# Local transformer: PE does two q projections of a later window pair ahead of the q.k products

## The chip, the cores and the metric

One NeuronCore of a Trainium2 chip runs the whole program. The metric is the time of one execution on the device, in microseconds (us). PE is TensorE (PEld its weight loads), DVE is VectorE, ACT is ScalarE, POOL is GpSimd, SP the engine that issues the DMAs.

## The reference, cut to what matters

A model of four blocks on x of shape (4, 512, 128); the change touches the third block's feed-forward part, a six-layer local transformer:

```python
DIM, DEPTH, HEADS, DIM_HEAD, WINDOW, QK_SCALE = 128, 6, 16, 64, 32, 8.0
def attn_layer(x, Wqkv, qs, ksc, Wo):
    q, k, v = split(x @ Wqkv)                     # 16 heads of 64
    q, k = l2norm(q) * qs, l2norm(k) * ksc
    q = q * cos * scale + rotate_half(q) * sin * scale
    k = k * cos / scale + rotate_half(k) * sin / scale
    out = local_attention(q, k, v)                # each window of 32 sees itself and the one before, masked
    return out @ Wo
def local_attention(q, k, v):
    sim = einsum('bhwie,bhwje->bhwij', q, k2) * QK_SCALE
    return einsum('bhwij,bhwje->bhwie', softmax(where(mask, -max, sim), -1), v2)
for i in range(DEPTH):
    x = attn_layer(shift_tokens(x), ...) + x
    x = ffn_layer(shift_tokens(x), ...) + x       # layernorm, W1, gelu gate, W2
```

## The kernel before

Each engine has its own in-order queue, written out by hand in `LocalTransformer` (L1612): `tensor` (L1688), `vector` (L1929), `scalar` (L2141), `gpsimd` (L2339) and `sync` (L2425). They meet only in semaphores.

The work of a layer is cut into two half-layers (two of the four batches each), hl = 0 to 11. A half-layer has four blocks u of 128 tokens for two batches, and each block gives two steps g: an even one for the block's windows 1 and 3, an odd one for windows 0 and 2. So a half-layer is eight steps, w = g mod 8, and there are 96 steps. In step g the engines are at different depths of a pipeline:

- PE turns p of g - 1 (`pe_turn_p`, L1820, banks 5 and 6), computes the scores of g (`pe_scores`, L1802: a mask matmul L1811 and 16 small ones L1814, for each of two windows, banks 3 and 4), projects q and k of g + 3 (`pe_rotate`, L1768, four calls i = 0 to 3 into banks 0, 1, 2 and 5; i = 0 and 1 are q, 2 and 3 are k), weighs the values with p of g - 1 (`pe_weigh`, L1831, called the second product), then the output projection of an even step (`pe_project`, L1861) or the value projection of the next block in an odd one (`pe_values`, L1781, L1786 its matmul), and turns q and k of g + 2 (`pe_by_feature`, L1790).
- VectorE copies half of p turned (L2089), takes each window's row maximum and subtracts it (`v_scores`, L2058, L2065 and L2070), multiplies the projections with the rotary tables (`v_rotate`, L1996, L2008 and L2013) and sums squares (L2020), scales q (L2055), sums p's rows and inverts (L2078, L2081).
- ScalarE copies the other half of p turned (L2283), squares the projections (L2229), takes Exp of the scores (L2174), copies the second product's results (L2292) and the values (L2239), places q and k turned (L2253, L2257), and in steps with MLP work does its copies and GELU (L2326, L2328, L2334). It also computes a first guess of roots (L2266, L2268; L2274, L2276 for the MLP).
- GpSimd adds the rotated halves (L2396), scales k (L2403), and scales p by the inverse sums (L2367), which is the event "soft" that `pe_turn_p` of the next step waits for.

The eight PSUM banks are all in use, and each PE call first waits until the bank's last reader is done (`self.freed`). Banks 0 and 1 are freed by ScalarE's placing copies of `pe_by_feature`. The scores wait for these copies too in an even step ("placed"), bank 3 in an odd step for VectorE's residual add (L2096).

The MLP of half-layer hl - 1 lies beside the attention of hl, by a table of places (`beside`, L1671). A place (w, 0) comes in PE's queue between the transposes of p and what the change reorders; the others come later. In w = 5 and w = 6 place (w, 0) turns the rows of the next half-layer (`pe_turn_x`, L1758, recorded at L270), and ScalarE's copies L2221 and L2222 give its columns, the event x_cols. The projections for a new half-layer's first block wait for it:

```python
        if i == 0 and t4 == 0:
            e.wait_ge(*s.at("x_cols", 2 * (2 * hl + bb) + 2))
```

Since the projections run three steps ahead, these are the ones issued in w = 5 and w = 6, each for the batch turned in that same step. The shift matmul of the MLP (`pe_shift`, L1881) ends w = 0; layer statistics (L2104) stand ahead of `v_scores` in w = 1; two MLP transposes (L1891) are in w = 2; MLP-up matmuls (L1902, L1905) in w = 2 to 5; the gate (L2132) ahead of `v_scores` in w = 4 and w = 5, and the down projection (L1917) later in these.

Of the kernel before, what the change touches and what calls it, by code (L numbers as in the profile page):

```python
# [273 lines left out]
def after(e, ends):  # L274
    for sem, value in ends:
        e.wait_ge(sem, value)


class Prologue:
# [61 lines left out]
    def tensor(self, e):  # L341
        pass
# [1269 lines left out]
class LocalTransformer:  # L1612
# [75 lines left out]
    def tensor(self, e):  # L1688
        K, s = self.K, self.s
        after(e, self.before)  # L1690
        e.wait_ge(*s.at("cleared", 3))
        self.freed = {k: [s.at("cleared", 3)] for k in range(8)}
        for bb in range(2):
            self.pe_turn_x(e, 0, bb, 6 + bb)
        for r in range(2):
            for i in range(4):
                self.pe_rotate(e, r, i)
        for n in range(4):
            self.pe_values(e, 0, n)
        for r in range(2):  # L1700
            for i in range(4):
                self.pe_by_feature(e, r, i)
        for i in range(4):
            self.pe_rotate(e, 2, i)
        for g in range(self.NG + 1):
            u, half = divmod(g, 2)
            hl, w = divmod(g, 8)
            this, last, turned, placed = g < self.NG, g >= 1, g + 3 < self.NG, g + 2 < self.NG
            if last:
                self.pe_turn_p(e, g - 1, 0)  # L1710
                self.pe_turn_p(e, g - 1, 1)
            if this:
                self.pe_beside(e, hl, w, 0)
                self.pe_scores(e, g, 0)
                self.pe_scores(e, g, 1)
            if turned:
                self.pe_rotate(e, g + 3, 0)
                self.pe_rotate(e, g + 3, 1)
            if last:
                self.pe_weigh(e, g - 1)  # L1720
            if turned:
                self.pe_rotate(e, g + 3, 2)
                self.pe_rotate(e, g + 3, 3)
            if this:
                self.pe_beside(e, hl, w, 1)
            if half == 0 and last:
                self.pe_project(e, u - 1)
            if half == 1 and this and u + 1 < self.NU:
                for n in range(4):
                    self.pe_values(e, u + 1, n)  # L1730
            if placed:
                for i in range(4):
                    self.pe_by_feature(e, g + 2, i)
            if this:
                self.pe_beside(e, hl, w, 2)
        f = self.NF - 1
        self.pe_shift(e, f)
        self.pe_turn(e, f, 0)
        self.pe_turn(e, f, 1)
        for n in range(6):  # L1740
            self.pe_up(e, f, n)
        self.pe_down(e, f, 0)
        self.pe_down(e, f, 1)
# [902 lines left out]
```

## Time and profile before

| | |
|---|---|
| median of 3 runs | 3143.26 us (3142.95 to 3143.5) |
| the profiled execution's own time | 3143.12 us |
| its span, first to last instruction | 3141.3 us |
| mean granted TensorE clock | 0.885 of full |
| PE busy over the span | 2442.7 us (78%) |
| DVE, ACT, POOL busy | 1963.5 us (63%), 1474.9 us (47%), 1031.8 us (33%) |
| transformer's 96 steps | about 735 to 2722 us |
| PE busy from 735 to 2722 us | 1771.43 of 1987.00 us |

A step is measured from the start of its transposes of p (the last half of them, where they come in two) to the next one's. In half-layer 4, with w = 0 and 1 of half-layer 5:

| w | length, us | end of p's scaling (L2367) to the next transposes, us |
|---|---|---|
| 2 | 19.9 | 0.2 |
| 3 | 19.3 | 2.7 |
| 4 | 25.1 | 5.8 |
| 5 | 23.0 | 2.2 |
| 6 | 17.7 | 0.05 |
| 7 | 16.25 | 0.05 |
| 0 | 21.3 (19.8 in six of eleven half-layers) | 5.1 |
| 1 | 21.5 | 1.3 |

Half-layers 1 to 10 repeat this to within a few tenths, save for w = 0 and what follows it. In half-layer 0, which has no MLP beside it, steps 2 to 4 and 7 take 16.2 to 16.3 us, and steps 5 and 6 take 17.6 and 16.4; the last column is 0.05 to 0.06 there throughout.

A line of the timeline gives the start, the length from first start to last end, the engine, the source line, what is written from what, how many instructions were merged into it, and in brackets how long the engine was idle before it and who ended that.

### The profile page before, as it was taken

To read this page: it belongs to the slowest core of one execution; us is meant where nothing else is said; L and a number is where in the kernel's file an instruction comes from. 1 tells how busy PE (TensorE), PEld (TensorE's weight loads), DVE (VectorE), ACT (ScalarE), POOL (GpSimd) and SP (SyncE) were. 2 spreads that over 40 slices of the span, in tenths; PEclk is the share of its full clock that TensorE was granted. 3 is DMA by queue.
4 is the path that set the end of the run, shared out by engine and by line. 5 is a ranking of instruction groups with operands and counts; after the bars stand their busy time and mean duration, and the time that the engine had idled before them with its cause. 6 is when DMAs were issued, how large, how long until landed. Compare 5 with 4: busy or idle time off the path is not lost. (4 is left out here: it accounts for less than half of the span.)

```text
span 3141.3 us, 71964 instructions
## 1 busy us (share of the span) xinstructions
PE 2442.7 (78%) x30424; PEld 1673.4 (53%) x30424; DVE 1963.5 (63%) x4358; ACT 1474.9 (47%) x2645; POOL 1031.8 (33%) x831
## 2 busy tenths in 40 slices
PE   6817758355889998998989898989898989758463
PEld 3515534233666666565656566656666666535252
DVE  4442235767887877777777868677868777234411
ACT  2303223423556566566656565656565656314120
POOL 0021220004544444444444434443444443000124
PEclk9958868658999999999999999999999999759676
DMA  7001100000101111102101110111100101020022
GB/s 259 3 18 51 34 15 1 0 1 24 29 25 28 53 29 32 29 15 59 29 25 29 53 36 25 28 53 29 32 15 25 35 25 29 15 82 2 9 64 57
DMA packets 71814, 110.10 MB, mean 35 GB/s; under 512 B 11394, under 2 KB 56712, under 8 KB 64966
## 3 DMA queue, kind: packets, MB, share of 16 engines
q1 hardware_dynamic: 67398, 97.88, 11.3%
q0 software_dynamic: 4096, 7.63, 0.8%
q8 instruction: 241, 3.95, 0.5%
q14 instruction: 79, 0.65, 0.1%
HBM read 42.29 MB, written 16.78 MB: 19 GB/s over the span
## 5 line engine op out<-in xcount | busy, mean ns | idle before, releaser
L2396 POOL TENSOR_TENSOR mem<-mem 128x512 f32<-128x512 f32 x384 | 468.0, 1228 | 938.4 <-DVE mem L2013 938.3
L2229 ACT ACTIVATE mem<-ps 128x512 f32<-128x512 f32 x384 | 216.5, 596 | 370.2 <-PE ps L1777 235.2
L1777 PE MATMUL ps<-mem 128*128 128x512 f32 x768 | 383.3, 622 | 4.3 <-DVE mem L2013 2.0
L2253 ACT ACTIVATE mem<-ps 64x512 f32<-64x512 f32 x384 | 228.7, 595 | 143.4 <-PE ps L1798 136.4
L2008 DVE TENSOR_TENSOR mem<-ps,mem 128x512 f32<-128x512 f32 x384 | 257.2, 670 | 22.9 <-ACT mem L2229 22.9
L2013 DVE TENSOR_TENSOR mem<-ps,mem 128x512 f32<-128x512 f32 x384 | 261.0, 680 | 0.0
L1786 PE MATMUL ps<-mem 128*128 128x512 f32 x384 | 208.6, 679 | 55.6 <-ACT mem L2239 55.6
L2020 DVE TENSOR_REDUCE mem<-mem 128x16 f32<-128x1024 f32 x192 | 232.4, 1210 | 0.0
L1848 PEld LDWEIGHTS ps<-mem 64*64 64x64 f32 x12288 | 190.7, 136 | 74.4 <-issue 73.0
L2403 POOL TENSOR_TENSOR mem<-mem 128x1024 f32<-128x1024 f32 x96 | 182.6, 1902 | 132.2 <-DVE mem L2055 132.2
L1814 PEld LDWEIGHTS ps<-mem 128*64 128x64 f32 x6144 | 194.7, 138 | 52.9 <-issue 52.9
L1814 PE MATMUL ps<-mem 128*64 128x64 f32 x6144 | 221.2, 225 | 0.0
L1798 PEld LDWEIGHTS ps<-mem 128*128 128x128 f32 x1536 | 184.7, 148 | 44.3 <-issue 43.6
L1848 PE MATMUL ps<-mem 64*64 64x32 f32 x12288 | 201.9, 220 | 3.5 <-issue 2.7
L1798 PE MATMUL ps<-mem 128*128 128x128 f32 x1536 | 195.5, 283 | 10.4 <-DVE mem L2013 9.7
L2089 DVE COPY mem<-ps 128x512 f32<-128x512 f32 x96 | 66.3, 690 | 217.6 <-PE ps L1826 217.6
L2367 POOL TENSOR_TENSOR mem<-mem 128x1024 f32<-128x1024 f32 x96 | 182.3, 1899 | 32.0 <-DVE mem L2081 32.0
L1777 PEld LDWEIGHTS ps<-mem 128*128 128x128 f32 x768 | 131.1, 190 | 111.7 <-issue 93.2
L1868 PEld LDWEIGHTS ps<-mem 128*128 128x128 f32 x1536 | 180.2, 194 | 19.3 <-issue 11.0
L1868 PE MATMUL ps<-mem 128*128 128x128 f32 x1536 | 181.7, 277 | 2.3 <-ACT mem L2292 2.3
L642 DVE TENSOR_REDUCE mem<-ps 128x8 f32<-128x616 f32 x96 | 76.5, 797 | 170.2 <-PE ps L493 170.2
L2065 DVE TENSOR_REDUCE mem<-ps 128x8 f32<-128x512 f32 x192 | 131.8, 686 | 74.2 <-PE ps L1814 74.0
(286 smaller groups left out, 4591.9 us busy)
## 6 DMA issues: line engine op xcount, KB each, us to landing
mem<-mem SPq DMA_DIRECT2D x48, 768.0 KB, 5.8
mem<-in_Wqkv SPq DMA_DIRECT2D x6, 1536.0 KB, 7.1
mem<-mem SPq DMA_DIRECT2D x36, 256.0 KB, 3.5
x<-mem SPq DMA_DIRECT2D x10, 512.0 KB, 6.5
mem<-x SPq DMA_DIRECT2D x16, 320.0 KB, 5.8
y<-mem SPq DMA_DIRECT2D x16, 320.0 KB, 2.5
mem<-in_W12T SPq DMA_DIRECT2D x8, 512.0 KB, 7.1
mem<-in_L3W SPq DMA_DIRECT2D x16, 256.0 KB, 5.4
```

The lines of the kernel that those rows point to most:

```text
L1777: e.matmul(self.K.ps[:, o, :], self.columns(u, bb), self.K.l2[l % 2]["Wqkv"][:, 512 * i:512 * i + 512], start=True, stop=True, skip_group_ ...
L1786: e.matmul(self.K.ps[:, k, :], self.columns(u, bb), self.K.l2[l % 2]["Wqkv"][:, 2048 + 512 * j:2560 + 512 * j], start=True, stop=True, ski ...
L1798: last = e.transpose(ps[:, o, 128 * c:128 * c + 128], self.T1[r % 2][k][:, h:h + 128], self.K.ident)
L1814: last = e.matmul(ps[64 * bb:64 * bb + 64, k, 64 * c:64 * c + 64], view(self.Qbd[ur][:, bb, c, wn], "p h q -> p (h q)"), self.kT[ur][:, bb ...
L1848: last = e.matmul(ps[64 * hp:64 * hp + 64, 7 - wi, at:at + 32], src[keys, bb, 128 * c + 64 * hp:128 * c + 64 * hp + 64], self.PT[keys, c, ...
L1868: last = e.matmul(ps[:, 3, 128 * bb:128 * bb + 128], self.oT[:, c, bb, :], self.K.l2[l % 2]["Wo"][:, c, :], start=c == 0, stop=c == 7, ski ...
L2008: e.tensor_tensor(h3(t1)[:, hh], src, bc(self.CT[:, t4, k, :], 1, 8), ALU.mult)
L2013: e.tensor_tensor(view(self.T2[:, 512 * j:512 * j + 512], "p (h a c) -> p h a c", h=8, a=2), swapped, bc(view(self.SN[:, t4, k, :], "p (a ...
L2020: e.tensor_reduce(self.ss[bb][:, H * k:H * k + H], h3(self.SQ), AX.X, ALU.add).then_inc(s("square_sums"), 1)
L2229: e.activation(self.SQ[:, 512 * j:512 * j + 512], self.K.ps[:, (0, 1, 2, 5)[i], :], ACT.Square).then_inc(s("squared"), 1)
L2253: e.activation(self.Qbd[ur][q, bb, 4 * j:4 * j + 4, :, hp, :], pv[q], ACT.Copy).then_inc(s("placed"), 1)
L2396: e.tensor_tensor(t1[:, cols], t1[:, cols], self.T2[:, cols], ALU.add).then_inc(s("rotated"), 1)
```

## The change

PE's queue alone is changed: in each step the calls i = 0 and 1 of `pe_rotate` move ahead of both `pe_scores`. Every instruction and every wait stays the same; each wait moves with its instruction.

```diff
             if this:
                 self.pe_beside(e, hl, w, 0)
-                self.pe_scores(e, g, 0)
-                self.pe_scores(e, g, 1)
             if turned:
                 self.pe_rotate(e, g + 3, 0)
                 self.pe_rotate(e, g + 3, 1)
+            if this:
+                self.pe_scores(e, g, 0)
+                self.pe_scores(e, g, 1)
             if last:
                 self.pe_weigh(e, g - 1)
             if turned:
```

## Rows read from the trace of the kernel before

**Rows 1.** The sum of waits, 735 to 2722 us: waiter, releaser, total us, times, longest
```profile
DVE mem L2065 <- PE ps L1814: 74.0, 51, 2.9
...
PE ps L1811 <- ACT mem L2257: 21.8, 25, 1.5
```

**Rows 2.** Timeline of step w = 7 of half-layer 4 and the start of w = 0
```profile
1547.42 1.09 PE L1826 MATMUL ps<-mem 128*128 128x128 f32 x8 [0.58 <-POOL mem L2367]
...
1548.92 0.38 PE L1811 MATMUL ps<-mem 128*128 128x512 bf16 x1 [0.41 <-DVE mem L2096]
...
1550.43 0.69 DVE L2065 TENSOR_REDUCE mem<-ps 128x8 f32<-128x512 f32 x1 [1.05 <-PE ps L1814]
...
1551.72 1.98 PE L1777 MATMUL ps<-mem 128*128 128x512 f32 x4
...
1553.58 0.69 DVE L2008 TENSOR_TENSOR mem<-ps,mem 128x512 f32<-128x512 f32 x1 [0.21 <-ACT mem L2229]
1553.63 2.07 PE L1848 MATMUL ps<-mem 64*64 64x32 f32 x128
...
1561.72 1.90 POOL L2367 TENSOR_TENSOR mem<-mem 128x1024 f32<-128x1024 f32 x1
...
1563.67 1.09 PE L1826 MATMUL ps<-mem 128*128 128x128 f32 x8 [0.70 <-POOL mem L2367]
...
1565.38 0.39 PE L1811 MATMUL ps<-mem 128*128 128x512 bf16 x1 [0.62 <-ACT mem L2257]
```

**Rows 3.** Timeline of step w = 6 of half-layer 4
```profile
1532.37 0.63 PE L270 MATMUL ps<-mem 128*128 128x128 f32 x4 [1.62 <-ACT mem L2257]
...
1532.83 0.38 PE L1811 MATMUL ps<-mem 128*128 128x512 bf16 x1
...
1533.71 0.59 ACT L2222 ACTIVATE mem<-ps 64x511 f32<-64x511 f32 x1
...
1534.34 0.69 DVE L2065 TENSOR_REDUCE mem<-ps 128x8 f32<-128x512 f32 x1 [2.87 <-PE ps L1814]
```

**Rows 4.** Timeline of the end of w = 0 and of w = 1, half-layer 5
```profile
1580.90 0.41 DVE L2096 TENSOR_TENSOR mem<-mem,ps 128x256 f32<-128x256 f32 x1
...
1581.90 2.04 PE L1881 MATMUL ps<-mem 128*128 128x512 f32 x2 [2.50 <-ACT mem L2257]
...
1584.99 1.04 PE L1826 MATMUL ps<-mem 128*128 128x128 f32 x8
...
1585.86 0.38 PE L1811 MATMUL ps<-mem 128*128 128x512 bf16 x1
...
1588.96 0.69 DVE L2065 TENSOR_REDUCE mem<-ps 128x8 f32<-128x512 f32 x1
...
1600.50 3.78 PE L1786 MATMUL ps<-mem 128*128 128x512 f32 x4 [4.23 <-ACT mem L2239]
```

**Rows 5.** Timeline of step w = 2 of half-layer 5
```profile
1616.38 1.07 ACT L2292 ACTIVATE mem<-ps 128x512 f32<-128x512 f32 x2
...
1617.39 1.04 PE L1891 MATMUL ps<-mem 128*128 128x128 f32 x8
```

**Rows 6.** Timeline of step w = 3 of half-layer 5
```profile
1635.60 1.09 ACT L2229 ACTIVATE mem<-ps 128x512 f32<-128x512 f32 x2 [0.40 <-DVE mem L2020]
...
1637.48 3.88 PE L1786 MATMUL ps<-mem 128*128 128x512 f32 x8
...
1646.08 0.66 PE L1826 MATMUL ps<-mem 128*128 128x128 f32 x4 [0.82 <-ACT mem L2326]
```

**Rows 7.** Timeline of step w = 4 of half-layer 5
```profile
1646.57 0.38 PE L1811 MATMUL ps<-mem 128*128 128x512 bf16 x1
...
1649.44 1.89 DVE L2132 TENSOR_TENSOR mem<-mem 128x512 f32<-128x512 f32 x3 [1.98 <-ACT mem L2334]
```

**Rows 8.** Busy time by stretch, w = 0 of half-layers 4 and 5 (stretch, length, PE, PEld, DVE, ACT, POOL busy, PE clock, DMA share, GB/s)
```profile
1400.40:1420.20 19.80, 16.69 (x262) 12.63 (x263) 14.82 (x24) 10.24 (x19) 10.62 (x9) 1.00 0.26 82
1563.67:1584.99 21.32, 18.20 (x263) 13.22 (x263) 14.83 (x24) 10.26 (x19) 10.62 (x9) 0.92 0.15 39
```

## The prediction

> **What bounds the kernel now.** I read three views: who waited for whom over the transformer's stretch, then the timeline of single steps, then granted clock by step. A step is one g of the loop; w is its place (0 to 7) in a half-layer hl (0 to 11), so there are 96 steps.
>
> The sum of waits [rows 1] says that VectorE waits 51 times, 74.0 us in all, for the q.k products, and that PE's first mask matmul of them waits for ScalarE. Both are in the loop that closes in a step with little else in it. Its timeline, w = 7 of half-layer 4 [rows 2]: PE starts the transposes of p at 1547.42, the scores at 1548.92, VectorE's first row maximum follows at 1550.43, and from there VectorE, then GpSimd, run without a gap that matters until p is scaled at 1561.72 + 1.90 = 1563.62. PE's next transposes start at 1563.67, having waited for exactly that. So the period of 16.25 us is a loop: transposes to scores 1.50, scores to maximum 1.51, maximum to p scaled 13.19, and 0.05. PE is busy most of it and still doesn't set it: it had waited 0.70 us when p arrived. Anything that delays the first score in such a step is paid in full.
>
> In other steps PE or ScalarE are late for other reasons, and a later score is free up to a slack that has to be read step by step. That is the whole question here, since the change alters no instruction, only PE's order: the two q projections of g + 3 (four matmuls, 1551.72 to about 1553.65, so 1.93 us [rows 2]) now run ahead of the scores of g. VectorE's, ScalarE's, GpSimd's and SP's queues keep their order, and no DMA moves. The second product starts after the same work as before.
>
> **Step by step.** The transposes take 0.90 us of PE's time (in w = 1, where nothing is waited for, 1584.99 to the scores at 1585.86 [rows 4], 0.87 and a little for the weight load). So in the new order scores start 0.90 + 1.93 = 2.83 us after the transposes, if banks 0 and 1 are free.
>
> *Plain odd steps* [rows 2]: before 1.50, because the scores' bank 3 waits for VectorE's residual add; now 2.83, so +1.33. Against that, VectorE had waited 0.21 us at its first rotate product for ScalarE's square of the same projection; that projection now comes early, and the 0.21 goes. Net +1.1. There are 13 (w = 7 of hl 1 to 10, three in hl 0, which has no MLP beside it): +14.3. The delay also reaches ScalarE's copies of the value products, but PE has the loop's wait to absorb that.
>
> *Plain even steps*: before 1563.67 to 1565.38 = 1.71, the scores waiting for ScalarE's last placing copy. The projections fill this wait instead. 2.83 - 1.71 - 0.21 = +0.9; two in hl 0: +1.8.
>
> *w = 6* [rows 3] is the dear one. Its projections belong to the next half-layer, so the first of them waits for x_cols, which ScalarE makes from transposes that PE does in the same step. These end on ScalarE at 1533.71 + 0.59 = 1534.30. Before, scores (from 1532.83) covered that. Now nothing does: projections from about 1534.4, scores at 1536.3, +3.5, less the 0.2, +3.3. VectorE was waiting for these scores (2.87 us idle), and p's loop closes this step too, so all of it is paid. In hl 0, w = 5 is the same (its MLP-up matmuls, which cover the wait in later half-layers, aren't there). 10 + 2 = 12 times: +39.6. Queued behind the waiting projection are the scores, both second-product groups and the rest of the step; VectorE, then ScalarE's Exp, then GpSimd wait for them.
>
> *w = 0* [rows 4]: same +0.9 on VectorE, but the end is PE's shift matmul, which waits for both ScalarE's copy (just before 1581.90) and VectorE's residual add (1580.90 + 0.41 = 1581.31). The add gets 0.9 later, so the shift about +0.5; 11 times: +5.5.
>
> *w = 1* [rows 4]: layer statistics stand ahead of the maximum on VectorE, so it starts 1588.96 - 1584.99 = 3.97 after the transposes; the first score now is there at 2.83 + 1.51 = 4.34. +0.35, and the chain through Exp to the MLP root carries it on; 11 times: +3.9.
>
> *w = 2* [rows 5]: PE is some 0.8 earlier, because projections fill its wait, but the MLP transposes (1617.39) then wait for ScalarE's output copies, whose last ends at 1616.38 + 1.07 = 1617.45. Gain 0.2; 11 times: -2.2.
>
> *w = 3* [rows 6]: PE-bound, with p scaled 2.7 us before PE comes to it (the table of steps), so the loop itself hides its +1.7. But ScalarE's squares of projections 2 and 3 wait for VectorE: from 1635.60 they go to 1637.3, take 1.09, then two MLP bias copies of 0.69 stand ahead of the first value copy, which starts at about 1639.7 and ends at 1640.3. PE's third value product, due at 1637.48 + 1.93 = 1639.4, needs that bank: +1.0. ScalarE's queue of copies then ends 1.1 later, and the second half of the next transposes (1646.08) waits for it. 11 times: +12.1.
>
> *w = 4 and w = 5* [rows 7]: VectorE does the MLP gate ahead of its maximum, until 1649.44 + 1.89 = 1651.33, which is 4.8 us after PE starts the scores (1646.57) where 1.5 would do: 3.3 us of cover for a delay of 1.9. Nothing. Were the gate gone, they would cost 1.1 each like the rest. Half-layer 11 has no more projections from w = 5 on: nothing.
>
> Sum: 14.3 + 1.8 + 39.6 + 5.5 + 3.9 - 2.2 + 12.1 = 75.0 us.
>
> **The clock.** At the end of w = 0 PE idles 2.50 us ahead of the shift [rows 4]. In five of the eleven half-layers the clock there fell to the lower of its levels (mean 0.92 to 0.95), and w = 0 took some 1.5 us more (21.3 against 19.8) [rows 8]. PE now arrives 0.5 or so earlier (its wait ahead of the scores is filled) and leaves 0.5 later, so it idles about 3.4 us. The unknown is how often the clock falls: bounds are no further case and all six left, 0 to +9; I take +7, since the idle time grows by a third and 4.23 us of idle in w = 1 was followed by value products at half speed (3.78 us for four, against 1.93) [rows 4]. The Trainium skill, TensorE: Matmul & The Clock Gate, section The HAM clock gate, says that the lower clock is the default and activity lifts it; by that rule the sum would go to the upper bound, +9. The trace agrees so far as these rows go.
>
> 75.0 + 7 = +82 on the profiled execution's 3143.12, hence 3225. The median of the runs shown, 3143.26, is the same to 0.01%.
>
> **Rivals.**
> 1. *The clock falls in w = 6 as well.* PE there idles 1.62 us, turns four blocks (0.63) [rows 3], and would idle 1.45 more. At half speed the projections take 1.9 more, and they are on the loop: 12 x 1.9 = 23, so 3248; with the scores slowed too, another 12 x 1 or so, 3260. For: the idle time is near that of w = 0. Against: there is work in the middle, and now, after 1.62 idle, the transposes run at full speed. Chance 0.25.
> 2. *The x_cols wait costs less than I say*, say because ScalarE gets to its two copies sooner, and w = 6 is like a plain step: 12 x (3.3 - 1.1) = 26 less, 3199. The queue order on ScalarE speaks against it. Chance 0.1.
> 3. *Faster: PE's queue is what binds.* If the wait of p's transposes for GpSimd [rows 2] were a coincidence of late PE work, filling PE's wait for ScalarE ahead of the scores would count, 21.8 us in all [rows 1]: 3121. It decides if PE's lag, not p, starts the transposes. It speaks against this that the start is 0.05 us behind GpSimd's end in w = 7 and w = 6 of every half-layer up to 10 (the table). Chance 0.04.
> 4. *The scores' delay is hidden*, VectorE catching up in w = 4 and 5 faster than read; within 0.2%. In the loop-bound steps there is nothing to catch up with. Chance 0.03.
>
> My forecast keeps 0.58. Its own unknowns (w = 3's 12, the clock's 0 to 9, the 0.2 a step) make it 3205 to 3235; taking in rivals 1 and 2, the range is 3192 to 3258. A measurement of this kernel can tell about 0.2%, 6.3 us. Faster 0.04, same 0.03, slower 0.93.
>
> **What would show it.** In w = 7 the scores start 2.83 us after the transposes and the period is 17.3 to 17.4 (16.25 before); VectorE's wait for the scores grows from 74 us to some 150 or more; ScalarE's second x_cols copy turns up as what ends PE's idle time ahead of the projections, 12 times; w = 6 takes 21.0 instead of 17.7 (the table); w = 4 and w = 5 keep their 25.1 and 23.0. Wrong would be: w = 7 unchanged (then the loop isn't one), a w = 6 of 19 or less, or a w = 4 or 5 that has moved by over 0.3.

## The result, and the profile after

| | before | after |
|---|---|---|
| median | 3143.11 us (4 runs, 3140.74 to 3143.5) | 3223.87 us (4 runs, 3221.21 to 3228.56) |
| profiled execution, its span | 3143.12, 3141.3 us | 3221.21, 3219.4 us |
| mean granted TensorE clock | 0.885 | 0.883 |

The ratio is 1.026, with an interval of 1.0242 to 1.0278: slower by 80.8 us between the medians, 78.1 between the profiled executions. The lines of the kernel after are one higher from L1714 on.

The first part of the page of after gives the busy time of the engines:

```profile
PE 2439.6 (76%) x30328; PEld 1682.3 (52%) x30424; DVE 1960.2 (61%) x4358; ACT 1467.4 (46%) x2645; POOL 1032.5 (32%) x831
```

The other engines differ from before by 8 us at most. PE shows 3 us less than before's 2442.7, but 96 of its records are missing, the first mask matmul of each step. Where these records exist they cover 20.3 us of PE's busy time in before, 21.8 in e1 and 14.2 in e4, so by an estimate from these figures PE was busy for 11 to 19 us more than before, and some 59 to 67 of the 78 us are idle time of PE. (The first record of the scores' products, L1815, stands for the start of the scores below.) The sum of waits over the transformer, 735 to 2801 us, in the columns of [rows 1], shows who waits:

```profile
DVE mem L2066 <- PE ps L1815: 174.0, 54, 9.0
...
PE ps L1882 <- DVE mem L2097: 28.1, 10, 3.1
...
PEld ps L1778 <- ACT mem L2223: 23.1, 23, 1.9
...
PE ps L1778 <- ACT mem L2223: 17.0, 13, 1.7
...
PEld ps L1812 <- ACT mem L2258: 1.8, 1, 1.8
```

VectorE's wait for the q.k products grew from 74.0 to 174.0 us [rows 1], the longest from 2.9 to 9.0. L2223 is ScalarE's copy into x_cols, and it ends 13 waits of PE ahead of the projections, 17.0 us: the 12 forecast, and one ahead of the first step. The placing copies can be compared at the weight load of the mask matmul alone, since the matmul's own records are missing. Before, it waited for them 37 times:

```profile
PEld ps L1811 <- ACT mem L2257: 35.0, 37, 1.8
```

and now once (the last row of the block above): the projections stand in these waits.

The timeline of w = 7 of half-layer 4 answers to [rows 2]:

```profile
1591.73 1.10 PE L1827 MATMUL ps<-mem 128*128 128x128 f32 x8 [1.00 <-POOL mem L2368]
...
1592.66 1.88 PE L1778 MATMUL ps<-mem 128*128 128x512 f32 x4
...
1594.69 1.15 PE L1815 MATMUL ps<-mem 128*64 128x64 f32 x32
...
1595.89 0.69 DVE L2066 TENSOR_REDUCE mem<-ps 128x8 f32<-128x512 f32 x1 [2.20 <-PE ps L1815]
...
1598.74 0.68 DVE L2009 TENSOR_TENSOR mem<-ps,mem 128x512 f32<-128x512 f32 x1
...
1606.87 1.90 POOL L2368 TENSOR_TENSOR mem<-mem 128x1024 f32<-128x1024 f32 x1
...
1608.83 1.09 PE L1827 MATMUL ps<-mem 128*128 128x128 f32 x8 [1.03 <-POOL mem L2368]
```

The projections now stand right behind the transposes, and VectorE's first row maximum comes 1595.89 - 1591.73 = 4.16 us after these start, where it was 3.01. From the maximum to p scaled it takes 12.88 us, where it was 13.19, and the rotate product no longer waits. So the period is 17.10 in place of 16.25, and PE, which waits 1.03 us for p at its end, still doesn't set it. When the scores start is seen in e2 (w = 7 of half-layer 4), where the mask matmul's records are there:

```profile
1553.96 1.09 PE L1831 MATMUL ps<-mem 128*128 128x128 f32 x8 [0.56 <-POOL mem L2372]
...
1556.61 0.38 PE L1816 MATMUL ps<-mem 128*128 128x512 bf16 x1
```

It is 2.65 us after the transposes, not 2.83.

In w = 6 the projections wait for x_cols. The timeline of half-layer 5 against [rows 3]:

```profile
1740.75 0.63 PE L270 MATMUL ps<-mem 128*128 128x128 f32 x4 [1.64 <-ACT mem L2258]
...
1742.09 0.59 ACT L2223 ACTIVATE mem<-ps 64x511 f32<-64x511 f32 x1
...
1742.73 1.98 PE L1778 MATMUL ps<-mem 128*128 128x512 f32 x4 [1.36 <-ACT mem L2223]
...
1746.06 0.69 DVE L2066 TENSOR_REDUCE mem<-ps 128x8 f32<-128x512 f32 x1 [6.22 <-PE ps L1815]
```

ScalarE's second copy ends at 1742.68, and 0.05 later the projections start; the maximum is there 5.31 us after L270 starts, 3.3 later than before. In half-layer 4 the same place looks like this:

```profile
1571.97 0.63 PE L270 MATMUL ps<-mem 128*128 128x128 f32 x4 [1.62 <-ACT mem L2258]
...
1573.96 3.55 PE L1778 MATMUL ps<-mem 128*128 128x512 f32 x4 [1.36 <-ACT mem L2223]
...
1578.98 0.69 DVE L2066 TENSOR_REDUCE mem<-ps 128x8 f32<-128x512 f32 x1 [7.90 <-PE ps L1815]
```

The waits are the same to 0.02 us, but the projections take 3.55 instead of 1.98: the clock has gone to its lower level. Busy time by stretch, in the columns of [rows 8], for w = 6 and w = 7 of half-layer 4 and w = 6 of half-layer 5:

```profile
1569.31:1591.73 22.42, 17.30 (x264) 12.71 (x263) 13.37 (x23) 11.04 (x21) 7.36 (x6) 0.92 0.19 48
1591.73:1608.83 17.10, 15.02 (x234) 9.79 (x235) 14.81 (x25) 10.71 (x21) 8.55 (x7) 1.00 0.01 2
1738.08:1758.82 20.74, 15.62 (x264) 12.17 (x263) 13.38 (x23) 11.56 (x22) 7.37 (x6) 1.00 0.21 52
```

At a clock of 1.00 w = 6 takes 20.74 us, with the fall 22.42, once 23.5. The clock fell in 7 of the 12 places where the projections wait. Two of the twelve are in half-layer 0: its w = 5 went from 17.20 to 19.47 us, its w = 6 from 16.82 to 21.10 with a fall. (The section on the profile before gives 17.6 and 16.4 for these two; the transposes start at 857.23, 874.43 and 891.25, which is 17.20 and 16.82.)

Step by step over all half-layers, from the start of the transposes to the next:

| steps | predicted, us | measured, us |
|---|---|---|
| plain odd, 13 | +14.3 | +11.4 (0.85 each) |
| plain even, 2 | +1.8 | +1.3 |
| w = 6, and w = 5 and 6 of half-layer 0 | +39.6 | +47.9 |
| w = 0 (delay, clock) | +5.5, +7 | -2.0 |
| w = 1 | +3.9 | -1.6 |
| w = 2 | -2.2 | +0.3 |
| w = 3 | +12.1 | +10.2 |
| w = 4 | 0 | +0.1 |
| w = 5 | 0 | +3.9 |
| outside these steps | 0 | +6.6 |
| sum | +82.0 | +78.1 |

Of the row "outside these steps", 5.8 us were there before the transformer began, in code that the change doesn't touch. That is one execution against one; such a difference is no effect of the change. After's profiled execution is also the fastest of its four.

### The profile page after: what moved, and what is told of

It is laid out like the page before. It is cut to its first block and busy times, and to the rows that moved or that the text cites. A ratio compares the mean times of both kernels' runs of the same rounds, so it can differ in the third digit from the quotient of the medians.

```text
span 3219.4 us, 71868 instructions
## 1 busy us (share of the span) xinstructions
PE 2439.6 (76%) x30328; PEld 1682.3 (52%) x30424; DVE 1960.2 (61%) x4358; ACT 1467.4 (46%) x2645; POOL 1032.5 (32%) x831
## 5 line engine op out<-in xcount | busy, mean ns | idle before, releaser
L1778 PE MATMUL ps<-mem 128*128 128x512 f32 x768 | 391.6, 635 | 23.9 <-ACT mem L2223 17.0
L1787 PE MATMUL ps<-mem 128*128 128x512 f32 x384 | 209.0, 675 | 80.0 <-ACT mem L2240 71.1
L2175 ACT ACTIVATE mem<-mem 128x1024 f32<-128x1024 f32 x96 | 101.6, 1058 | 308.1 <-DVE mem L2071 308.1
L1815 PEld LDWEIGHTS ps<-mem 128*64 128x64 f32 x6144 | 195.8, 138 | 86.0 <-issue 86.0
L2066 DVE TENSOR_REDUCE mem<-ps 128x8 f32<-128x512 f32 x192 | 131.7, 686 | 174.3 <-PE ps L1815 174.0
L1815 PE MATMUL ps<-mem 128*64 128x64 f32 x6144 | 222.3, 226 | 16.7 <-issue 1.9
```

Source lines behind the costliest of these rows:

```text
L1778: e.matmul(self.K.ps[:, o, :], self.columns(u, bb), self.K.l2[l % 2]["Wqkv"][:, 512 * i:512 * i + 512], start=True, stop=True, skip_group_ ...
L1787: e.matmul(self.K.ps[:, k, :], self.columns(u, bb), self.K.l2[l % 2]["Wqkv"][:, 2048 + 512 * j:2560 + 512 * j], start=True, stop=True, ski ...
L1815: last = e.matmul(ps[64 * bb:64 * bb + 64, k, 64 * c:64 * c + 64], view(self.Qbd[ur][:, bb, c, wn], "p h q -> p (h q)"), self.kT[ur][:, bb ...
```

## The experiments

Each ratio is to the kernel before in the same series: its median was 3142.5 us for e1 to e4 (15 runs), 3143.94 for e5 to e8 (35 runs, 3139.2 to 3160.54) and 3143.3 for e9 (14 runs). What is said of steps comes from one profiled execution of each kernel. Those of e3 (3169.09), e5 (3156.02) and e7 (3157.86) lie 7 to 14 us above their medians, so they may show more falls of the clock than most. Lines behind the edit in `tensor` are five higher in e1 to e4 and e6 to e9 than in before (L1782 is the projection, L1777 in before); in e5 they are not shifted, save for the scaling of p, L2365.

| run | median, us (range, runs) | ratio, interval |
|---|---|---|
| after | 3223.87 (3221.21 to 3228.56, 4) | 1.026, 1.0242 to 1.0278 |
| e1: new order in w = 5, 6 | 3205.95 (3202.16 to 3209.39, 5) | 1.0202, 1.0189 to 1.0215 |
| e2: new order in the others | 3169.95 (3162.7 to 3184.34, 6) | 1.0093, 1.0075 to 1.0111 |
| e3: new order in "free" steps | 3155.01 (3143.02 to 3169.26, 10) | 1.0037, 1.0021 to 1.0053 |
| e4: after, wait filled | 3209.11 (3203.19 to 3213.9, 5) | 1.0211, 1.0198 to 1.0224 |
| e5: p scaled first | 3142.04 (3134.83 to 3156.02, 12) | 0.9983, 0.9966 to 1.0 |
| e6: one projection ahead | 3145.03 (3134.7 to 3160.91, 12) | 1.0007, 0.9989 to 1.0026 |
| e7: split, "free" steps | 3150.74 (3140.32 to 3157.86, 11) | 1.0012, 0.9997 to 1.0028 |
| e8: p scaled first, one ahead in w = 2 | 3146.68 (3140.25 to 3154.22, 11) | 1.0011, 0.9998 to 1.0024 |
| e9: p scaled first, one ahead | 3136.43 (3127.07 to 3147.28, 11) | 0.9974, 0.9957 to 0.9991 |

**The wait for x_cols alone (e1), and everything but it (e2).** The two halves of the change, by a condition on the step (e2 has `w not in (5, 6)`):

```diff
+            ahead = w in (5, 6)
+            if turned and ahead:
+                self.pe_rotate(e, g + 3, 0)
+                self.pe_rotate(e, g + 3, 1)
             if this:
                 self.pe_scores(e, g, 0)
                 self.pe_scores(e, g, 1)
-            if turned:
+            if turned and not ahead:
```

> The new order only in w = 5 and w = 6, the steps whose projections wait for x_cols; the old order in the other six. Theory (the wait, plus the clock that falls behind it): w = 6 takes 20.7 to 20.8 us with the clock up and 22.4 with it down, half-layer 0 pays in w = 5 too, w = 5 of half-layers 1 to 10 is free. 12 x 3.0 for the wait and 1.7 each for some 6 or 7 falls of the clock: +46 to +50 on the kernel before, about 3191. Rival (a later score costs the same in every step, 78 us over 95 steps): 22 steps x 0.82 = +18, about 3161. Rival (the wait but no clock): +36, 3179.

> The complement: the new order everywhere but in w = 5 and w = 6. Theory: 0.85 in each plain odd step (13), 0.65 in each plain even one (2), 0.9 in w = 3 (11), nothing in w = 4, about nothing in w = 0 to 2: +22 to +26, about 3167; w = 6 keeps 17.7. Rival of equal cost: 73 steps x 0.82 = +60, 3203.

e1 took 63 us more than the kernel before (3142.5 in that series), e2 27. Busy time by stretch, w = 6 and w = 7 of half-layer 4, first of e1:

```profile
1548.84:1572.31 23.47, 18.64 (x264) 13.66 (x262) 13.36 (x23) 11.53 (x22) 7.36 (x6) 0.85 0.19 46
1572.31:1588.55 16.24, 15.14 (x234) 9.63 (x234) 14.90 (x25) 10.21 (x20) 8.55 (x7) 1.00 0.01 2
```

and then of e2:

```profile
1536.26:1553.96 17.70, 15.51 (x264) 12.15 (x262) 13.44 (x23) 10.51 (x20) 7.34 (x6) 1.00 0.24 61
1553.96:1571.06 17.10, 15.16 (x234) 9.79 (x234) 14.82 (x25) 11.02 (x22) 8.56 (x7) 1.00 0.01 2
```

The steps separate cleanly: in e1 w = 7 keeps the old 16.24 and w = 6 has all of the delay, in e2 w = 6 keeps 17.70 and w = 7 has 17.10. e1's excess is in w = 6: the clock stayed up in one of ten (20.73), was 0.92 in two (22.1) and 0.85 or 0.86 in seven (23.5). So e1 missed its 3191 by 15 us: the wait was as expected, the falls were more and longer (10 of 12 places against after's 7). e2 came within 3 us of its 3167. Together they make 91, more than the 81 of after: the twelve steps that wait cost 59.9 us in e1's profiled execution and 47.9 in after's. The wait itself is 3.0 in both.

**The steps that should be free (e3).** `ahead = hl >= 1 and w in (0, 1, 2, 4, 5)`, otherwise as e1.

> The new order only in steps where the prediction found a later first score covered or nearly so: w = 0, 1, 2, 4 and 5 of half-layers 1 to 11. Theory: within 4 us of the kernel before (3139 to 3147), w = 4 and 5 keep 25.1 and 23.0. The prediction as it stood had +0.5, +0.35 and -0.2 for w = 0, 1, 2 and +7 for the clock in w = 0: +14, 3157. Rival of equal cost: 54 x 0.82 = +44, 3187.

3155.01, 12.5 us more than before's: more than the expected 4, and near the +14 of the prediction, though in part for another reason. In the profiled execution w = 4 took 25.1 and w = 5 took 23.0 as in before, save for three w = 5 (half-layers 2, 7, 9) of 27.68 at a clock of 0.82, and the clock fell in w = 0 in all eleven half-layers (21.2 to 21.7 us), where before has five. Of the 25.9 us by which this execution is longer than before's, w = 0 makes 10.7 and w = 5 makes 13.1, for which the prediction had nothing. The stretch of one w = 0:

```profile
1404.78:1426.22 21.44, 18.06 (x263) 13.16 (x264) 14.72 (x24) 10.03 (x19) 10.61 (x9) 0.93 0.34 104
```

PE is busy for 18.06 against the 16.69 of a w = 0 at 1.00 [rows 8]. With the clock down before's w = 0 takes 21.32 and e3's 21.44; with it up before's takes 19.80 and after's 19.92. So the order costs 0.1 there, and the rest is how often the clock falls.

**Filling the wait (e4).** The kernel after, with one more matmul in w = 6 between the x_cols transposes and the projections. It writes bank 0, which the first projection then overwrites, so it adds PE work and nothing else:

```diff
+            if turned and w == 6:
+                after(e, self.freed[0])
+                e.matmul(self.K.ps[:, 0, :], self.K.ident, self.K.l2[0]["Wqkv"][:, 0:512], start=True, stop=True,
+                         skip_group_check=True)
             if turned:
                 self.pe_rotate(e, g + 3, 0)
```

> The changed kernel with one more 128x512 matmul (two instructions, 0.95 us) issued into bank 0 in w = 6 between the transposes and the projection that waits for x_cols; its result is overwritten by that projection. The wait stays (1.36 us idle before), so without an effect on the clock the time is that of the changed kernel, 3224. Theory (idling there is what lets the clock fall, 1.7 us each time): w = 6 takes 20.7 in all or nearly all half-layers, 7 x 1.7 = -12 us, about 3212. Rival (it falls for another reason): 3224 within 2; if the extra matmul got in the way, slower.

3209.11, 15 us less than after, with more work on PE; 3212 was expected. The timeline of w = 6, half-layer 4, and its busy time by stretch:

```profile
1561.75 1.02 PE L1716 MATMUL ps<-mem 128*128 128x512 f32 x2
...
1563.27 1.98 PE L1782 MATMUL ps<-mem 128*128 128x512 f32 x4 [0.50 <-ACT mem L2227]
```

```profile
1558.63:1579.35 20.72, 16.72 (x267) 12.61 (x265) 13.37 (x23) 11.54 (x22) 7.36 (x6) 1.00 0.21 52
```

The extra matmul takes 1.02 us and leaves 0.50 of the wait of 1.36, the projections run in 1.98, and w = 6 takes 20.7 in all ten half-layers, with no fall of the clock in any, where after has 6 in ten and e1 has 9. Nor is the profiled execution an exception: the granted clock over the whole program is 0.885 to 0.889 in e4's five executions and 0.881 to 0.884 in after's four. That settles the rival about w = 6: the falls there come with PE idle in the wait, and the delay by ScalarE's copy alone is worth 3.0. The total proves less than the steps do. Between the two profiled executions the twelve steps that wait give 12.8 us, and w = 5 gives 4.5, but w = 0 to 2 take 9.3 back, and 9.4 come from ahead of the first transposes of p.

**The loop, shortened elsewhere (e5).** If GpSimd's scaling of p closes the loop, doing it sooner must shorten w = 7 with PE's order as before. In gpsimd():

```diff
-            if turned:
-                self.p_rotate(e, g + 3, 2)
...
+            if turned:
+                self.p_rotate(e, g + 3, 2)
```

so that the rotary add of projection 2 stands behind the scaling.

> The kernel before, PE's order untouched; on GpSimd alone the scaling of p goes ahead of the rotary add of projection 2. It tests the loop from its other end. Theory (in plain steps p's scaling releases PE): the scaling starts when the inverse sums are there, 1561.15 in w = 7 of half-layer 4, and not behind the add at 1561.72: -0.5 in 14 plain odd steps, -0.3 in 13 plain even ones, together -11, about 3131; w = 7 takes 15.75. Rival (PE's own queue sets these steps): 3142, w = 7 stays at 16.25.

The timeline of w = 7 of half-layer 3 and the start of w = 0:

```profile
1389.67 1.09 PE L1826 MATMUL ps<-mem 128*128 128x128 f32 x8 [0.28 <-POOL mem L2365]
...
1403.47 1.90 POOL L2365 TENSOR_TENSOR mem<-mem 128x1024 f32<-128x1024 f32 x1 [0.71 <-DVE mem L2081]
...
1405.43 1.09 PE L1826 MATMUL ps<-mem 128*128 128x128 f32 x8 [0.21 <-POOL mem L2365]
...
1407.63 0.39 PE L1811 MATMUL ps<-mem 128*128 128x512 bf16 x1 [1.11 <-ACT mem L2257]
```

The period is 15.76, 0.49 less, and PE again starts on GpSimd's end (1405.37). So p's loop is what bounds, which rules out rival 3, that PE's queue does. The total is a miss: 3131 was expected, and 3142.04 can't be told from no change. Plain odd steps gave 6.5 us and w = 6 gave 2.8, as expected, but w = 0 paid most of it back: the last line is the next step's first mask matmul, which waits 1.11 us for ScalarE's placing copies (0.62 in [rows 2]), and w = 0 took 20.3 at the full clock, 0.5 more than before (with the clock down 21.8 against 21.3). A gain in front of a step that is bounded by something else is lost there.

**One projection ahead (e6).** PE waits 0.41 us for the scores' bank [rows 2]; one projection fits into about that:

```diff
+            ahead = w not in (5, 6)
+            if turned and ahead:
+                self.pe_rotate(e, g + 3, 0)
             if this:
                 self.pe_scores(e, g, 0)
                 self.pe_scores(e, g, 1)
-            if turned:
+            if turned and not ahead:
                 self.pe_rotate(e, g + 3, 0)
+            if turned:
                 self.pe_rotate(e, g + 3, 1)
```

> Half the change: only one q projection ahead of the scores (not in w = 5 and 6), the other behind them as before. Theory: the scores start 0.90 + 0.96 = 1.86 us after the transposes against 1.50 (odd) and 1.71 (even), less the 0.3 that VectorE's first rotary product gains: w = 7 16.3, w = 3 19.3 to 19.4 (no stall of the value products), so within 4 us of the kernel before, 3142. Rival (the cost goes with the projections moved): half of the 27 us of the run without w = 5 and 6, 3156.

3145.03, as expected. w = 7 kept 16.25 and w = 3 took 19.38; the plain even steps of half-layer 0 took 16.05, 0.2 less. The cost isn't proportional to the work moved ahead: half of it costs nothing, the other half 0.85 a step.

**Splitting the two (e7).** e6's edit with e3's condition, against the idea that four long matmuls in a row, followed by nothing but small ones, let the clock fall in w = 5.

> The steps of the run with the free steps (w = 0, 1, 2, 4, 5 of half-layers 1 to 11), but one projection ahead of the scores and one between them and the second product. Idle times of PE are nearly those of that run. Theory (scores and second product back to back, small matmuls only, are what lets the clock fall in w = 5, 4.7 us each time): no fall in w = 5, and a median of 3142 to 3149 instead of 3155. Rival (the falls in w = 5 come with the new order as such, or by chance): some w = 5 at 27.7, median near 3155.

3150.74. Three w = 5 (half-layers 1, 3, 7) took 27.67, as many as in e3. The idea fell.

**Shorter loop and one ahead in w = 2 alone (e8).** e5's edit with e6's, `ahead = hl >= 1 and w == 2`.

> The scaling of p first on GpSimd, and one projection ahead of the scores in w = 2 alone, where PE waits 1.3 us for ScalarE ahead of the scores. Theory: the first alone gives about -11; in w = 2 PE comes earlier but then waits for ScalarE's output copies, so at most 0.2 x 11 = 2 more: 3129 to 3132. Rival (PE's earlier arrival in w = 2 counts in full, 0.8 each): 3123.

A miss: 3146.68, no gain. It told something else: one w = 5 (half-layer 1) took 27.67 at 0.81 though this kernel has the old order in w = 5. So that fall doesn't need the new PE order in the step it is in.

**Both small edits (e9).** e5's and e6's: the projection ahead fills the 1.11 us into which e5's gain had gone.

> Both small changes together: p's scaling first on GpSimd, and one q projection ahead of the scores in all steps but w = 5 and 6. With the scaling alone, w = 7 fell to 15.76 but the even step behind it rose (w = 0 from 19.8 to 20.3, the plain even ones of half-layer 0 from 16.25 to 16.45), because its scores wait for ScalarE's placing copies, which had not moved. Theory: one projection fits into that wait, and VectorE's 0.3 comes on top: plain even steps 16.1 or less, plain odd 15.8, w = 7 15.76, w = 6 17.4; some 8 us less than before, 3134 to 3138, if the clock falls as often. Rival (the two don't add up, the even steps stay at 16.45): 3142.

3136.43 against 3143.3 in that series, 0.9974 with an interval below 1: better than both kernels. The timeline of w = 0 of half-layer 4 and what follows:

```profile
1395.38 1.09 PE L1831 MATMUL ps<-mem 128*128 128x128 f32 x8 [0.54 <-POOL mem L2370]
...
1397.25 0.39 PE L1816 MATMUL ps<-mem 128*128 128x512 bf16 x1
...
1412.91 1.10 PE L1886 MATMUL ps<-mem 128*128 128x512 f32 x2 [2.50 <-ACT mem L2262]
...
1414.49 1.04 PE L1831 MATMUL ps<-mem 128*128 128x128 f32 x8
```

The mask matmul comes 1.87 us after the transposes (2.20 in e5) with no wait ahead of it, and the step takes 1414.49 - 1395.38 = 19.11, where it took 19.80 in before [rows 8] and 20.3 in e5. The plain even steps of half-layer 0 took 15.8, w = 6 17.4 as expected; w = 7 took 15.94 and not 15.76. This step at the full clock is one of two among eleven; in the others the clock fell, and the interval is wide, since the falls differ from run to run.

## Why the prediction was right, and where its steps were not

The forecast was 3225 with a range of 3192 to 3258; 3223.87 was measured. The mechanism holds, but that the total came within 2 us is luck: +82.0 predicted and +78.1 in the profiled execution are made of errors of both signs (the table of steps). w = 6 cost 8.3 more than its term, w = 0 to 2 cost 17.5 less, and 6.6 came from outside the steps, most of it by chance.

**The loop**, from which all else follows, was read rightly. e1 and e2 move w = 7 and w = 6 one without the other, e5 shortens w = 7 from GpSimd's end, and PE waits for p in each. The transposes-to-maximum time was put at 4.34 and is 4.16, since the scores start after 2.65 and not 2.83; what VectorE gains behind the maximum was put at 0.21 and is 0.3. So a plain step costs 0.85, not 1.1.

**w = 6, the term that was mis-sized.** "+3.3" a step: 3.0 with the clock up (2.3 in w = 5 of half-layer 0), by the very wait that was named, 1.36 us for ScalarE's second x_cols copy. What was missing is the clock: it fell in 7 of 12 places at 1.6 to 2.8 us each, 12.8 in all, and so 47.9 were measured in place of 39.6. This was rival 1, at 0.25, and it came true in part: "now, after 1.62 idle, the transposes run at full speed" was no evidence for two idle times close behind one another. e4 shows the cause by taking away two thirds of the second one. Why it fell in six of the half-layers 1 to 10 and not in the other four, with the same two idle times, stays open.

**w = 0 to w = 2, the step that was wrong.** The prediction took +5.5 for the delay, +7 for the clock, +3.9 and -2.2, in all +14.2. Measured: -2.0 - 1.6 + 0.3 = -3.3. e2 and e4, with the new order in the same steps, have +2.1 and +6.0 there, in one execution each. The idle time did grow, by the mechanism named; the timeline of w = 0 in after, half-layer 5, against [rows 4]:

```profile
1626.68 0.41 DVE L2097 TENSOR_TENSOR mem<-mem,ps 128x256 f32<-128x256 f32 x1
...
1627.14 1.13 PE L1882 MATMUL ps<-mem 128*128 128x512 f32 x2 [3.07 <-DVE mem L2097]
```

It is 3.07 in place of 2.50, ended by VectorE's residual add (1627.09), no longer by ScalarE's copy. But the step got 0.1 longer, not 0.5 (19.92 against 19.80). The add ends 1627.09 - 1608.83 = 18.26 after the transposes, 0.6 later than before's 1581.31 - 1563.67 = 17.64 and not 0.9, and about as much had been slack against ScalarE's copy (1581.90). And "the idle time grows by a third", so the clock falls oftener, was the failed inference. In before the idle time ahead of the shift is 2.50 us in all eleven half-layers, and the clock fell in five; in e1 it is 2.50 as well, with the old order in w = 0, and it fell in eight. In after it is 3.06 or 3.07 in nine, and it fell in one of them ahead of the shift (half-layer 4) and in two within the step's last 0.5 us (7 and 10); in half-layer 3 it fell 9 us into the step, behind another idle time, and the shift's was 2.49. In e3 it fell in all eleven. So the length of this idle time doesn't say whether the clock falls; what decides it no run here shows. The Trainium skill, TensorE: Matmul & The Clock Gate, section The HAM clock gate, says that the lower clock is the default and activity lifts it; by that rule the prediction's sum would have gone to its upper bound. e4 agrees with it in w = 6 (an added matmul of 1.02 us, and none of ten falls); w = 0 of after doesn't, with more idle time and no more falls.

In w = 1 the first maximum was to come 0.35 later and came 0.13 later (4.10 after the transposes in half-layer 5, 3.97 before). That would make w = 1 longer, not 1.6 shorter. The clock falls in w = 1 in all eleven half-layers of both kernels, for different lengths of time (0.82 to 0.85 of full before, 0.84 to 0.92 after), and that an effect of the order is in it isn't shown. I count w = 0 to 2 as one sum for that reason.

**w = 3** has the right size and the right queue, but the wrong wait. The timeline of after, half-layer 4, against [rows 6]:

```profile
1511.53 1.02 PE L1787 MATMUL ps<-mem 128*128 128x512 f32 x2
1512.23 0.69 ACT L2327 ACTIVATE mem<-ps,mem 128x512 f32<-128x512 f32 x1
1512.80 0.70 ACT L2329 ACTIVATE mem<-ps,mem 128x512 f32<-128x512 f32 x1
1513.37 0.62 ACT L2240 ACTIVATE mem<-ps 128x512 f32<-128x512 f32 x1
1513.56 2.94 PE L1787 MATMUL ps<-mem 128*128 128x512 f32 x6 [1.01 <-ACT mem L2329]
```

The value products break into 2 and 6 records, with 1.01 us of idle time where +1.0 was expected. A value product is two records, and the four go to banks 3, 4, 3, 4; so it is the second that waits, not the third. What it waits for is bank 4, which the second MLP bias copy (L2329, until 1513.50) has yet to read, and not bank 3, which the first value copy (until 1513.99) would free for the third product. The sum of waits shows it at the weight load of this product, once for each of the 11 steps:

```profile
PEld ps L1787 <- ACT mem L2329: 17.9, 11, 1.8
```

Both waits come from the same late start of ScalarE's queue, behind its squares, so the size was right though the named wait wasn't. The step is 0.9 longer, 10.2 in all.

**w = 4 and w = 5** kept 25.1 and 23.0 by the cover named, VectorE's gate: both e3 and after show it. One w = 5 of after (half-layer 9) took 27.68, which by the prediction's own sign (a move of over 0.3) speaks against it; its clock was at 0.82, and what else is known of it stands below. Rivals 2 to 4 fell: w = 6 is dearer than a plain step by 2.2 us at the same clock, e5 bounds PE out, and w = 7 took its delay in full.

## What to carry to other kernels

Where a loop through several engines sets the period, first find its members and the slack of each step, then ask of reordered work on one engine only how much later it makes the loop's member: half of the same move was free here and the other half cost 0.85 us a step. A moved instruction brings its own wait along, and on an in-order queue that wait is paid by all that stands behind it; look where the moved work first touches data made in the same step. Idle time on TensorE ahead of loop-bound matmuls may cost again through the clock, in some executions of it and not in others: give such a term a range, don't take its sign from one idle time, and if the wait can't go, try to fill it.

## What was not expected of the hardware

The clock also fell while PE was busy. The timeline of w = 5 in after, half-layer 9:

```profile
2400.86 0.91 PE L1918 MATMUL ps<-mem 128*128 128x128 f32 x6 [0.74 <-ACT mem L2293]
...
2403.39 1.43 PE L1918 MATMUL ps<-mem 128*128 128x128 f32 x6
...
2407.77 6.73 PE L1787 MATMUL ps<-mem 128*128 128x512 f32 x8
```

and the busy time by stretch, of the step (here from the first half of its transposes, which come in two) and of parts of it:

```profile
2386.99:2416.09 29.10, 27.05 (x275) 17.25 (x275) 15.93 (x27) 16.98 (x29) 9.28 (x7) 0.82 0.00 1
```

```profile
2402.00:2404.00 2.00, 2.00 (x14) 1.65 (x13) 2.00 (x2) 1.09 (x2) 1.02 (x1) 0.92 0.00 0
2404.00:2406.00 2.00, 2.00 (x8) 1.55 (x8) 2.00 (x4) 0.00 (x0) 1.82 (x1) 0.50 0.00 0
2406.00:2414.00 8.00, 8.00 (x16) 3.85 (x15) 3.73 (x7) 1.79 (x3) 4.96 (x5) 0.51 0.00 0
2414.00:2416.00 2.00, 2.00 (x18) 1.71 (x17) 0.00 (x0) 1.43 (x3) 0.00 (x0) 1.00 0.00 0
```

PE is busy without a gap from 2402, and the clock is at 0.50 from about 2403.8 to 2413.9; the eight value-product records take 6.73 where other half-layers show 3.88. The step from transposes to transposes is 27.68 in place of 23.00. In half-layers 1 to 10 it was seen once in after, three times each in e3 and e7, once each in e6, e8 and e9, and in none of before, e1, e2, e4 and e5, in one execution of each. But in w = 5 of half-layer 11, which has no projections, the clock is low in all eleven kernels. In before, behind idle times of 1.19 and 2.88 us:

```profile
2674.87 6.54 PE L1786 MATMUL ps<-mem 128*128 128x512 f32 x8
```

```profile
2666.00:2680.00 14.00, 14.00 (x38) 9.18 (x38) 1.41 (x3) 1.24 (x3) 3.73 (x3) 0.50 0.00 1
```

There too PE is busy without a gap for 14 us at half the clock, and the step takes 29.75 us. So the kernel before has such a stretch of its own. e8 shows that the new order within w = 5 isn't needed for the other kind, and e7 that splitting the projections doesn't prevent it. Its cause stays open; it is worth 4.7 us each time and part of why e3 was dearer than its order. The page of the Trainium skill named above warns, in its section Seeing it yourself, that a trace's records of the clock have been unreliable, and that the clock was seen stuck at a quarter for over 50 us. These rows show neither: the value products do take longer where the clock reads 0.50 (6.73 and 6.54 us against 3.88), and it reads a half, for some 10 us in the one case and at least 14 in the other.
